# One block for the context and shared stages of a two-layer mixture kernel, token tiles loaded by groups, variance sums on VectorE

## The reference

```python
x = x + xattn(layernorm(x), token_ids, ctx, ctx, ctx)
x = x + ffn(layernorm(x), ...)

def xattn(h, token_ids, Wg, Wu, Wd):            # Wg = Wu = Wd = ctx, 4 experts of 512 x 512
    expert = minimum(clip(token_ids, 0, 24999) // 6250, 3)
    # each token: y = (silu(h @ Wg[e].T) * (h @ Wu[e].T)) @ Wd[e].T, with e its expert

def ffn(h, ...):                                # 32 experts, inner width 256
    n = rmsnorm(h) * norm_w
    scores = softmax(n @ gate_w.T); top 4, weights normalised
    routed = sum over the 4 chosen experts of weight * (silu(g) * u) @ w2[e],  g, u = split(n @ w13[e])
    shared = (silu(n @ sg) * (n @ su)) @ sd
    return h + routed + shared
```

## Time and profile before

| | |
|---|---|
| median of 3 runs | 687.01 us (685.64 to 691.67) |
| profiled execution | 690.36 us |
| its span, first to last instruction | 688.6 us |
| TensorE busy | 628.3 us (91%) |
| VectorE busy | 440.4 us (64%) |
| ScalarE busy | 366.9 us (53%) |
| GpSimd busy | 331.9 us (48%) |
| mean granted TensorE clock | 0.984 |

### The profile page before, as it was taken

One profiled execution on the slowest core, in us unless ns is written; L12 is line 12 of the kernel. 1 busy time (PEld: TensorE's weight loads), 2 busy tenths in 40 slices (PEclk: granted clock), 3 DMA queues, 4 the chain that ended last, 5 costly groups with the idle time before them and its releaser, 6 DMA issues.

```text
span 688.6 us, 15278 instructions
## 1 busy us (share of the span) xinstructions
PE 628.3 (91%) x3242; PEld 508.5 (74%) x3243; DVE 440.4 (64%) x1024; ACT 366.9 (53%) x637; POOL 331.9 (48%) x374
## 2 busy tenths in 40 slices
PE   1699999967989998899999999999999999999990
PEld 1578877856868886688878887788788788787870
DVE  6668777763899996555666656665565665655630
ACT  5366666644534222455675656655556655656530
POOL 3637766661011113454564554555555546465542
PEclk9999999997999999999999999999999999999996
DMA  6512223434875544677798897997768998987645
GB/s 267 165 48 63 100 104 122 164 126 145 311 211 121 149 70 77 165 197 206 192 267 213 213 276 212 284 283 201 204 187 215 273 269 203 280 212 204 108 65 70
DMA packets 35790, 124.69 MB, mean 181 GB/s; under 512 B 4784, under 2 KB 5936, under 8 KB 31152
## 3 DMA queue, kind: packets, MB, share of 16 engines
q0 software_dynamic: 24256, 59.26, 39.1%
q1 hardware_dynamic: 11504, 65.09, 26.8%
HBM read 90.51 MB, written 39.06 MB: 188 GB/s over the span
## 4 chain that ended last, share of the span: by engine, by line
PE 33%; DMA 22%; issue 8%; DVE 5%; POOLq 2%; ACT 2%; POOL 2%; DVEq 1%; ACTq 0%; SPq 0%
DMA out<-r_oh,e_sidx 10%; PE sps_gu L223 6%; PE sps_gu L225 6%; PE sps_gu L224 6%; DMA out<-r_rank,e_sidx 5%; DMA out<-normw,e_sidx 3%; DMA raw<-in_experts_w 3%; PE sps_t L223 2%; PE sps_t L225 2%; PE sps_t L224 2%; PE sps_table L993 1%; PE sps_rank L938 1%; PE sps_table L938 1%; PE sps_cols L938 1%; POOLq L924 1%
## 5 line engine op out<-in xcount | busy, mean ns | idle before, releaser
L1347 DVE TENSOR_TENSOR wl<-raw,wh x87 | 105.9, 1227 | 58.3 <-ACT wh L1134 55.3
L223 PE MATMUL sps_gu<-wh,s_xth 128*128 x320 | 132.6, 414 | 3.0 <-DVE s_xtl L1330 2.6
L225 PE MATMUL sps_gu<-wh,s_xtl 128*128 x320 | 125.9, 393 | 0.0
L224 PE MATMUL sps_gu<-wl,s_xth 128*128 x320 | 125.1, 391 | 0.0
L926 POOL DMA_INDIRECT out<-r_oh,e_sidx x40 | 69.4, 1736 | 93.2 <-DMA out<-r_rank,e_sidx 40.0
L1134 ACT ACTIVATE wh<-raw x87 | 91.2, 1061 | 17.4 <-issue 9.7
L914 POOL DMA_INDIRECT both<-hb_dram,e_gidx x76 | 82.3, 1083 | 31.3 <-issue 18.9
L1109 ACT ACTIVATE both<-sps_gu 128x256 f32<-128x256 f32 x80 | 30.7, 384 | 81.3 <-PE sps_gu L225 81.2
L223 PEld LDWEIGHTS sps_gu<-wh,s_xth 128*128 128x128 f32 x320 | 60.2, 188 | 14.7 <-issue 4.6
L225 PEld LDWEIGHTS sps_gu<-wh,s_xtl 128*128 128x128 f32 x320 | 60.0, 188 | 13.9
L223 PE MATMUL sps_t<-wh,s_ath 128*128 x160 | 69.5, 435 | 0.5
(11 more groups left out here) (319 smaller groups left out, 1429.7 us busy)
## 6 DMA issues: line engine op xcount, KB each, us to landing
raw<-in_experts_w SPq DMA_DIRECT2D x32, 1536.0 KB, 8.0
craw<-in_ctx_w SPq DMA_DIRECT2D x4, 1024.0 KB, 7.7
both<-hb_dram SPq DMA_DIRECT2D x16, 256.0 KB, 3.6
out<-hb_dram SPq DMA_DIRECT2D x4, 1024.0 KB, 17.9
out<-both POOLq DMA_DIRECT2D x16, 256.0 KB, 4.0
both<-hb_dram,e_gidx POOLq DMA_INDIRECT x76, 5.8
out<-r_oh,e_sidx POOLq DMA_INDIRECT x40, 5.5
sraw<-in_sg SPq DMA_DIRECT2D x1, 512.0 KB, 5.5
```

Of the source, the lines that this page charges most:

```text
L223: pe.matmul(acc, left_hi, right_hi, start=start, stop=False)
L224: pe.matmul(acc, left_hi, right_lo, start=False, stop=False)
L225: return pe.matmul(acc, left_lo, right_hi, start=False, stop=stop)
L1347: dve.tensor_tensor(m.wl[:, w, ROWS[part], :], m.raw[:, bass.ds(x % 2, 1), ROWS[part], :], m.wh[:, w, ROWS[part], :].bitcast(F32), ALU.sub ...
```

## The change

The two stages share one block, so no barrier lies between them, and the context stage's semaphores are kept through both. SP no longer waits for all stores before it loads token tile 4: it works out how far each of the first three groups of four token tiles reaches, and waits at tiles 4 and 8 for the stores of the context tiles that the group needs, and at tile 12 for all. On TensorE the wait for all x2 and the 24 small matmuls behind it are gone from the end of the context stage; it waits for all x1 before it turns tile 2, and issues 48 small matmuls behind tile 3. ScalarE's first Exp moves behind the high part of tile 3. VectorE makes both variance sums in one instruction of 128 x 2 behind the aggregate (L731), from two small constant tensors, and GpSimd's two instructions for them (L434, L435) are gone.

```diff
--- before.py
+++ after.py
+GROUPS = G // RING - 1
...
+        m.top = top
+        m.block = top.enter_context(nc.Block())
...
-        s = semaphores(nc, st, "c_", (
+        s = m.c = semaphores(nc, m.top, "c_", (
...
-        ps_spread = ps_prefix[0:1, P:2 * P]
+        ps_spread = ps_prefix[0:1, P:(1 + GROUPS) * P].rearrange("p (q n) -> p q n", q=GROUPS)
...
-        spread = sb("spread", [P, 3])
+        spread = sb("spread", [P, GROUPS])
+        furthest = sb("furthest", [1, 2, GROUPS])
...
+        slope = sb("slope", [P, 2])
+        offset = sb("offset", [P, 2])
...
-        block = st.enter_context(nc.Block())
+        block = m.block
...
@@ context, SP
-            reach_of_first = sp.value_load(m.tab1[0:1, 1, 1:2], min_val=2, max_val=MAX1)
+            m.reach = [sp.value_load(m.tab1[0:1, 1, 1 + q:2 + q], min_val=2, max_val=MAX1) for q in range(GROUPS)]
...
-            sp.wait_ge(hbs[0], 16 * ((reach_of_first + 1) // 2))
-            sp.wait_ge(hbs[1], 16 * (reach_of_first // 2))
+            sp.wait_ge(hbs[0], 16 * ((m.reach[0] + 1) // 2))
+            sp.wait_ge(hbs[1], 16 * (m.reach[0] // 2))
...
@@ context, GpSimd, "rstd2"
-                    var = mv[:, 1, t.par, 1:2]
-                    nc.gpsimd.tensor_scalar(rs2[:, t.par, 0:1], var, 1.0, LN_EPS, ALU.mult, ALU.add)
-                    nc.gpsimd.tensor_scalar(rs2[:, t.par, 1:2], var, 1.0 + RMS_EPS, RMS_EPS * LN_EPS, ALU.mult, ALU.add).then_inc(s["var2"], 1)
                     pool.wait_ge(s["var2"], t.n + 1)
...
@@ context, TensorE
-            pe.matmul(ps_spread, spread[:, 0:1], m.ident[:], start=True, stop=True).then_inc(m.s["spread_row"], 1)
+            for q in range(GROUPS):
+                mm = pe.matmul(ps_spread[:, q], spread[:, q:q + 1], m.ident[:], start=True, stop=True)
+            mm.then_inc(m.s["spread_row"], 1)
...
-            pe.wait_ge(s["x2"], 2 * number_of_pairs(pe, m.tab1[0:1, 1, 0:1], MAX1))
-            keep_busy(pe, m, ps_z[0], WARM)
+            m.pe_tiles = 2 * pairs
...
@@ context, VectorE
+            dve.memset(slope[:, 0:1], 1.0)
+            dve.memset(slope[:, 1:2], 1.0 + RMS_EPS)
+            dve.memset(offset[:, 0:1], LN_EPS)
+            dve.memset(offset[:, 1:2], RMS_EPS * LN_EPS)
...
-            dve.tensor_reduce(spread[:, 0:1], sel[:, 1, 0:RING], AX.X, ALU.max).then_inc(m.s["spread"], 1)
+            dve.tensor_reduce(spread[:], sel[:, 1, 0:GROUPS * RING].rearrange("p (q r) -> p q r", r=RING), AX.X, ALU.max).then_inc(m.s["spread"], 1)
...
-                            k(dve.tensor_reduce(spread[0:1, 1:2], ps_spread, AX.X, ALU.max))
-                            k(dve.tensor_scalar(spread[0:1, 2:3], spread[0:1, 1:2], 1.0, 2.0, ALU.add, ALU.max))
-                            dve.tensor_copy(m.tab1[:, 1, 1:2], spread[0:1, 2:3]).then_inc(m.s["early"], 1)
+                            k(dve.tensor_reduce(furthest[:, 0], ps_spread, AX.X, ALU.max))
+                            k(dve.tensor_scalar(furthest[:, 1], furthest[:, 0], 1.0, 2.0, ALU.add, ALU.max))
+                            dve.tensor_copy(m.tab1[:, 1, 1:1 + GROUPS], furthest[:, 1]).then_inc(m.s["early"], 1)
...
                     dve.bn_aggr(mv[:, 1, t.par, :], stat[:, 1, t.par, :]).then_inc(s["mv2"], 1)
+                    dve.wait_ge(s["mv2"], t.n + 1)
+                    wait(dve, s["affine"], t.n - 1)
+                    m.carry(dve)
+                    dve.scalar_tensor_tensor(out=rs2[:, t.par, 0:2], in0=slope[:], scalar=mv[:, 1, t.par, 1:2], in1=offset[:],
+                                             op0=ALU.mult, op1=ALU.add).then_inc(s["var2"], 1)
...
@@ shared, SP
-            for q in ("stored0", "stored1"):
-                sp.wait_ge(m.s[q], 16 * pairs)
             for i in range(RING, G):
+                if i % RING == 0 and i // RING < GROUPS:
+                    sp.wait_ge(m.s["stored0"], 16 * ((m.reach[i // RING] + 1) // 2))
+                    sp.wait_ge(m.s["stored1"], 16 * (m.reach[i // RING] // 2))
+                elif i % RING == 0:
+                    for q in ("stored0", "stored1"):
+                        sp.wait_ge(m.s[q], 16 * pairs)
                 wait(sp, s["t1"], i - RING + 1)
                 sp.dma_start(xg[:, i % RING], m.hb_dram[i * P:(i + 1) * P, 0:D]).then_inc(gx[i % RING], 16)
...
@@ shared, TensorE
             for q in range(G // 2):
                 for i in (2 * q, 2 * q + 1):
+                    if i == 2:
+                        pe.wait_ge(m.c["x1"], m.pe_tiles)
                     pe.wait_ge(gx[i % RING], 16 * (i // RING + 1))
                     wait(pe, s["t1lo"], i - RING + 1)
                     turn(turned[i % RING], xg[:, i % RING], C).then_inc(s["t1"], 1)
+                if q == RING // 2 - 1:
+                    keep_busy(pe, m, ps_gu[1], 2 * WARM)
                 if q >= 1:
                     logits(q - 1)
...
@@ shared, ScalarE
-            nc.scalar.activation(prob[:, 0, 0, 0:2], m.minus_half[:], ACT.Exp)
             for q in range(G // 2 + 3):
                 if q < G // 2:
                     for i in (2 * q, 2 * q + 1):
                         act.wait_ge(s["t1"], i + 1)
                         nc.scalar.activation(turned_hi(i).rearrange("p c n -> p (c n)"), turned[i % RING][:], ACT.Copy).then_inc(s["t1hi"], 1)
+                if q == RING // 2 - 1:
+                    nc.scalar.activation(prob[:, 0, 0, 0:2], m.minus_half[:], ACT.Exp)
                 if 1 <= q <= G // 2:
                     act.wait_ge(s["logits"], q)
```

## The result

| | before | after |
|---|---|---|
| median, same chip and time | 690.66 us (10 runs) | 684.39 us (10 runs, 681.77 to 687.25) |
| ratio after / before | | 0.9913 (95%: 0.9891 to 0.9936) |
| profiled execution (span) | 690.36 (688.6) | 682.47 (680.8) |
| expert stage's first warming matmuls start at | 273.65 | 267.65 |

The change makes the kernel faster by 0.9%, some 6.0 us. The forecast was 678.9, from 674.5 to 683.5: the direction is right, the time lies 0.9 us outside. Two things make up the distance of 5.5 us. The kernel before gave a median of 690.66 where the forecast started from 687.01: 3.65. And the medians lie 6.27 apart instead of 8.1: 1.8. That second part looks like a small slip in one term. It is not: three terms were wrong by 2.2 to 2.6 us each, one too low and two too high.

A forecast was written before the change was run, and what follows sets the result against it. The prediction saw the 150 to 165 us hole between context and shared stages as the two-block cost, and GpSimd pacing the context loop. 6.6 + 0.5 + 1.0 = 8.1 us gained, giving 678.9 us; range 674.5 to 683.5.

The forecast's parts named there:

- The seam, 6.6: Between context and shared stages: in one block ScalarE starts `t1hi(0)` right after its last context pass, gaining 6.6 us.
- The tail, 1.0: Last three context tiles pass GpSimd faster without its two variance instructions: 1.0 us gained, between 0 and 1.6.
- The steady loop, 0.5: Context loop: GpSimd saves 0.52 us a tile, but a VectorE hold leaves some 0.1; 0.5 us taken, bounds 0 and 3.3.
- the first rival: Context loop: GpSimd's relief comes through whole, TensorE sets 6.40 us a tile; gain 10.9, time 676.1 us; chance 0.2.
- the test that I named: GpSimd's round: 6.8 us with L440 or L441 of 0.6 to 0.7 proves the lock, 6.4 disproves it.
- The loads, 0: Seam: token tiles 4 to 15, now queued by SP in the second block, arrive before TensorE needs them; cost 0.
- the cap that I had named for the tail: Landing of the store two tiles back, which ScalarE's base pass also needs, limits the tail's gain, taken as 1.0 us.
- The clock, 0: Seam: TensorE's clock stays high through 3.6 us of new idle, having fallen only behind 5 us before; cost 0.
- the second rival: The clock falls in the new idle or the seam keeps a cost: 2.5 us lost, 681.4 us; chance 0.13.
- The table load, 0: ScalarE's Exp table load, 1.28 us, moved behind the fourth `t1hi`: cost 0.3 us at most, taken as 0.
- The warming: 48 small matmuls behind turn 3 take 2.7 or 5.5 us by clock level, ending before the first logits at 157.9.
- The two signs: Seam: wrong if the first `t1hi` trails ScalarE's last pass by over 0.5 us, or TensorE awaits a load among the logits.

The follow-up runs named there:

- x1: The changed kernel with both variance instructions back on GpSimd and VectorE's one removed; ratio 0.9968 to the kernel before, median 689.64 us.
- x2: The kernel before, two blocks kept, with only the variance sums moved to VectorE; ratio 0.9905 to the kernel before, median 684.82 us.
- x3: The changed kernel, but token tiles 4 and on load only when 16 context tiles are stored; ratio 0.9845 to the kernel before, median 680.32 us.
- x7: The changed kernel with norm weights copied once to PSUM, so VectorE's hn product has one SBUF input; ratio 0.9929 to the kernel before, 685.61 us.
- x12: As x3, but the wait stands before token tile 6, so two loads run beside store 15; ratio 0.9881 to the kernel before, 682.29 us.
- x4: The changed kernel with 96 warming matmuls instead of 48; ratio 0.9901 to the kernel before, median 683.21 us.
- x11: As x3, with the Exp and its table load ahead of the first `t1hi`; ratio 0.9905 to the kernel before, median 683.75 us.
- x8: The changed kernel without the 48 warming matmuls; ratio 0.9924 to the kernel before, median 685.58 us.
- x10: The changed kernel with the edits of x3 and x7 together; ratio 0.9866 to the kernel before, median 680.24 us.
- x9: The changed kernel, but token tile 4 waits for all context stores, so no grouping; ratio 0.9899 to the kernel before, median 684.36 us.

## Why the prediction came out as it did

**The seam, 6.6: right.** `t1hi(0)` follows ScalarE's last pass with no gap, and without the wait for the store x1 gives 6.7.

**The tail, 1.0: right.** x2 shows it alone: 1.0. With both parts and no delay of the store x3 gives 7.8, where the two terms make 7.6.

**The steady loop, 0.5: wrong, it is 3.1.** The failed step is the sentence that of 0.52 us "some 0.1 is left". The hold itself was foreseen to the place: L440, now L443, was to begin at +2.06 from the store's issue and be held to about +2.5; it began at 97.39 - 95.36 = +2.03 and ended at +2.67. The error is what follows. I added the hold to the round as if the gather moved with it. The evidence against it stood in the earlier trace rows: GpSimd had 0.56 us of idle time ahead of the gather, for its waits. That time does not stay when an instruction ahead of it is held longer: x7 shows it at 0.49 to 0.55 without the hold, and it is 0.17 with it. So the first rival, which takes the relief whole, was right here, and the test that I named (a held instruction of 0.6 to 0.7 "proves the lock", a round of 6.4 "disproves it") was badly made: both came.

**The loads, 0: wrong, 2.4.** The failed step is "Cost 0; if the store were later than that, TensorE would wait for it". I looked at the loads as something that waits for stores, and asked whether they come in time. They did. I didn't ask what they do to the stores in flight. Four loads of 256 KB, two ahead of a store issued at 148.37 and two behind it, stretch its landing from 3.5 to 6.3 us, and that landing was the cap that I had named for the tail. x3, x12 and the change give 0, 0.71 and 2.45 us of wait for none, two and four loads. The Trainium skill (DMA: Bandwidth & Descriptors, Queues, rings and completion order) says that each DMA engine takes turns between the queues that have work for it; the traces agree in this, that the store lands later the more loads the other queue has in flight; no run shows the turns themselves.

**The clock, 0: wrong, 2.2.** I took the high level because the new idle time was to be 3.6 us. With the store's delay it was 5.67, and the second rival's 2.5 us came as 2.2. x4 takes these away and nothing else. But my reason, that it had fallen only behind 5 us, would not have carried either: in x12 it fell 3.5 us behind the last product, in x11 2.0.

**The table load, 0: right.** Moved behind the fourth `t1hi` it costs nothing; x11 puts it back on the path and pays 1.5, and 1.9 more of clock.

**The warming: covered, as forecast,** but with little effect in the change (0.5, x8, hardly beyond the scatter).

**The sum.** Of the profiled execution: 0.2 lost at the start (which starts vary by), 3.1 in the loop, 7.7 in the seam and tail, less 2.4 for the store and 2.2 for the clock, is 6.0. Forecast for the last four were 0.5, 7.6, 0 and 0. The loop's term was 2.6 too low and the other two together 4.6 too high, so that they cancel in part. A sum only 2 us off with three wrong terms is luck. The range, made around the terms' own doubts, didn't hold the other 3.65 us: the median of three runs of the kernel before was lower than those of the later ones, which lie from 689.62 to 691.78. From 690.66 the same gain of 8.1 would have made 682.6.

**The two signs behind "I am wrong if"** saw none of the three. The first `t1hi` follows ScalarE's last pass at once and TensorE waits for no load in the stretch of logits, in the change as in the forecast. The clock's row and the loop's pace, which I had also named, did show two of them. The delay of the store stood ahead of ScalarE's last pass, where I had named no sign.

## What to carry to other kernels

When a transfer is moved earlier, ask whose landing it delays, not only whether it arrives in time: a buffer released by a DMA is on the path as much as an instruction. Idle time that is put down to the issue of waits can hide a stall of the instruction ahead of it, so a stall is not added to a round without checking what stands behind it. And price the seam of two stages with the clock in it: where 3.1 us of idle time had left the clock up (x3), 1.5 us more on the path cost 3.4 (x11).

## What the runs showed of the hardware that was not expected

The idle time after which the granted clock falls is no single number here. The levels are 1.00 (2.4 GHz) and 0.50 (1.2 GHz); the moment of a fall is worked out from the mean of the slice of 1 or 2 us that holds it. Behind TensorE's last product the clock fell after 2.0 us in x11, 2.8 in x7, 3.4 in x1, 3.5 in x12, 3.8 in the change, 4.0 in x8 and 5.1 in the kernel before. In x10, x3 and x4 TensorE stood idle for 2.95, 3.12 and 3.13 us and it didn't fall. What TensorE did before does not sort these. In x11, x3 and x9 it does the same up to 152.1 or 152.2, to within 0.1 us: 48 small matmuls as the last work. In x11 the clock fell at about 154.2 (the mean of 154 to 155 us is 0.58). In x3, where TensorE stands until 155.28, it didn't fall. In x9, whose first 156 us are those of x3, it fell at about 156.5, in the middle of the work that had begun at 155.24. This window of x9 shows it, columns as above.

```profile
156.00:157.00 1.00, 0.98 (x8) 0.51 (x5) 0.37 (x1) 0.82 (x2) 0.00 (x0) 0.76 0.23 78
```

Work just begun doesn't keep the clock by itself. What decides between x3, x9 and x11 is open: one trace of each was taken, and a repeat of the same kernel could come out the other way.
